# Softplus by Tanh and Ln, the gate's shares by Tanh, in a planned two-stream mixture-of-experts kernel

## The reference

```
q = softplus(gelu(x @ q_w1.T + q_b1) @ q_w2.T + q_b2)      # k likewise
z = 1 / (sum over c of q*k_sum * SCALE + dim);  A = q^T k;  out = (A v^T * SCALE + v) * z
...
top_val, top_idx = top_k(xf @ gate_w + gate_b, 2)          # 24 experts
prob = softmax(top_val)                                    # two numbers per token
out += prob[expert] * (gelu(xf @ w1 + b1) @ w2 + b2)       # exact gelu, per expert
```

## Time and profile before

| | us |
|---|---|
| three runs, median (lowest to highest) | 1048.32 (1047.94 to 1048.72) |
| span of the profiled execution | 1043.2 |
| PE busy | 905.4 (87%) |
| PE weight loads busy | 789.0 (76%) |
| DVE busy | 569.7 (55%) |
| ACT busy | 484.6 (46%) |
| POOL busy | 497.2 (48%) |

### The profile page before, as it was taken

One profiled execution on the slowest core, in us unless ns is written; L12 is line 12 of the kernel. 1 busy time (PEld: TensorE's weight loads), 2 busy tenths in 40 slices (PEclk: granted clock), 3 DMA queues, 4 the chain that ended last, 5 costly groups with the idle time before them and its releaser, 6 DMA issues.

```text
span 1043.2 us, 26677 instructions
## 1 busy us (share of the span) xinstructions
PE 905.4 (87%) x8696; PEld 789.0 (76%) x8696; DVE 569.7 (55%) x2226; ACT 484.6 (46%) x814; POOL 497.2 (48%) x519
## 2 busy tenths in 40 slices
PE   4757999998999799999999998996899999998670
PEld 2327899976889777899888898883688867888570
DVE  7897500066785065785058400588883888872112
ACT  3333544448634257734345444352528455654320
POOL 0551560271027571035372743577744657277655
PEclk9886999999999899999999999898999999999985
DMA  9765999973578783488895899944658456669982
GB/s 306 242 205 156 300 308 242 237 203 95 123 191 231 187 212 104 118 208 234 218 254 146 209 274 226 230 129 130 153 141 189 124 115 165 142 155 247 258 196 75
DMA packets 278655, 200.19 MB, mean 192 GB/s; under 512 B 146112, under 2 KB 233536, under 8 KB 278400
## 3 DMA queue, kind: packets, MB, share of 16 engines
q1 hardware_dynamic: 262144, 164.90, 63.1%
q0 software_dynamic: 16384, 33.59, 11.2%
HBM read 115.56 MB, written 55.57 MB: 164 GB/s over the span
## 4 chain that ended last, share of the span: by engine, by line
PE 58%; DVE 20%; DMA 8%; issue 5%; ACT 4%; POOL 4%; SPq 1%; DVEq 0%; POOLq 0%; ACTq 0%
PE bank L1425 20%; PE bank L1403 5%; PE bank L1405 5%; PE bank L1404 5%; DMA turned<-rows 4%; PE bank L1291 4%; POOL got L2123 3%; PE bank L1244 3%; DMA got<-y_l,slot_index 3%; PE bank L1263 2%; PE bank L1220 2%; PE bank L1253 2%; PE bank L1422 2%; DVE xn L1708 2%; PE bank L1301 2%
## 5 line engine op out<-in xcount | busy, mean ns | idle before, releaser
L1425 PE MATMUL bank<-second,hid 128*128 128x128 f32 x2560 | 369.7, 287 | 0.0
L2123 POOL DMA_INDIRECT got<-y_l,slot_index x256 | 244.7, 956 | 236.4 <-DMA y_l<-y 114.3
L1425 PEld LDWEIGHTS bank<-second,hid 128*128 128x128 f32 x2560 | 324.7, 195 | 4.7 <-issue 3.0
L2103 POOL DMA_INDIRECT rows<-rows_sent,slot_index x192 | 187.8, 978 | 282.2 <-issue 167.7
L1575 ACT ACTIVATE hid<-bank 128x512 f32<-128x512 f32 x320 | 189.7, 597 | 280.4 <-PE bank L1405 266.0
L1403 PE MATMUL bank<-turned,blocks_l 128*128 128x128 f16 x1280 | 239.7, 222 | 41.1 <-DMA turned<-rows 31.2
L1921 DVE SCALAR_TENSOR_TENSOR x_res<-got,share,x_res 128x128 f32<-128x128 f32 x256 | 77.4, 348 | 319.5 <-DMA got<-y_l,slot_index 312.9
L1405 PE MATMUL bank<-turned,blocks_l 128*128 128x128 f16 x1280 | 239.8, 223 | 0.0
L1404 PE MATMUL bank<-turned,blocks_l 128*128 128x128 f16 x1280 | 239.1, 222 | 0.0
L1403 PEld LDWEIGHTS bank<-turned,blocks_l 128*128 x1280 | 127.6, 100 | 55.4 <-issue 52.7
L1404 PEld LDWEIGHTS bank<-turned,blocks_l 128*128 x1280 | 127.1, 99 | 8.9 <-issue 5.9
(11 more groups left out here) (208 smaller groups left out, 1215.6 us busy)
## 6 DMA issues: line engine op xcount, KB each, us to landing
second<-in_w_dram SPq DMA_DIRECT2D x243, 256.0 KB, 5.3
y_l<-y SPq DMA_DIRECT2D x104, 256.0 KB
second<-in_w_dram SPq DMA_DIRECT2D x192, 128.0 KB
got<-y_l,slot_index POOLq DMA_INDIRECT x256
rows<-set SPq DMA_DIRECT2D x1, 3584.0 KB, 14.9
rows<-set SPq DMA_DIRECT2D x7, 512.0 KB, 6.4
rows<-rows_sent,slot_index POOLq DMA_INDIRECT x192
hid<-in_w_dram SPq DMA_DIRECT2D x9, 256.0 KB, 5.2
```

What stands on the lines that cost most here:

```text
L1425: m = t.do.matmul(out, hid[:, at], second[:, at], start=False, stop=(c == C - 1))
L2103: d = g.do.indirect_dma_start(rows_dram[s], at, rows[:, 2 * D * i:2 * D * i + 2 * D], None)
L2123: d = g.do.indirect_dma_start(got_mem[slot][:, col:col + D], None, y_dram[layer][s][layer.team(ev.i)], at)
```

## The change

Three things change, and the planner's table with them.

The softplus is computed as max(x, 0) - ln(0.5 - 0.5 t) with t = tanh(-|x|/2), which is the same number, since 0.5 - 0.5 t = 1/(1 + exp(-|x|)). The gap's softmax of two is computed from the Tanh of half the gap; the four DVE instructions of the shares become two. The constant 0.5 gets a column of its own among the constants. The planner's costs of ACT fall from 5.0 to 3.7 for `la_soft` and from 1.6 to 0.35 for `r_gap`, that of DVE for `r_share` from 0.8 to 0.5.

```diff
-CCOL, CCOLS = columns([("ident", P), ("rev0", L0.E), ("rev1", L1.E), ("iota", 1), ("one", 1),
+CCOL, CCOLS = columns([("ident", P), ("rev0", L0.E), ("rev1", L1.E), ("iota", 1), ("one", 1), ("middle", 1),
...
-        "r_top": [[(VE, 1.0 + 5 * n, 0.1)]], "r_gap": [[(VE, 0.2, 0.1), (SC, 1.6, 0.1)]],
+        "r_top": [[(VE, 1.0 + 5 * n, 0.1)]], "r_gap": [[(VE, 0.2, 0.1), (SC, 0.35, 0.1)]],
...
-        "r_share": [[(VE, 0.8, 0.1)]], "r_end": ...
+        "r_share": [[(VE, 0.5, 0.1)]], "r_end": ...
...
-        "la_second": [[(PE, 2.4, 0.2), (VE, 1.4, 0.1)]], "la_soft": [[(SC, 5.0, 0.15), (VE, 1.4, 0.1)]],
+        "la_second": [[(PE, 2.4, 0.2), (VE, 1.4, 0.1)]], "la_soft": [[(SC, 3.7, 0.15), (VE, 1.4, 0.1)]],
...
-                a.do.activation(gap, gap, ACT.Exp).then_inc(gap_exp[ev.s].sem, 1)
+                a.do.activation(gap, gap, ACT.Tanh, scale=0.5).then_inc(gap_tanh[ev.s].sem, 1)
...
-                    a.do.activation(mag, mag, ACT.Exp).then_inc(attn_exp[ev.s].sem, 1)
+                    a.do.activation(mag, mag, ACT.Tanh, scale=0.5).then_inc(attn_exp[ev.s].sem, 1)
...
-                    a.do.activation(mag, mag, ACT.Ln, bias=ccol("one")).then_inc(attn_exp[ev.s].sem, 1)
+                    a.do.activation(mag, mag, ACT.Ln, bias=ccol("middle"), scale=-0.5).then_inc(attn_exp[ev.s].sem, 1)
...
-                    gap, total = columns["gap"], columns["pick"]
-                    v.wait_ge(*gap_exp[ev.s].after(Ev("r_gap", *ev[1:])))
-                    then(v.do.tensor_scalar(total, gap, 1.0, None, ALU.add))
-                    then(v.do.reciprocal(total, total))
-                    then(v.do.tensor_scalar(S[:, 0, :], total, 0.5, None, ALU.mult))
-                    m = v.do.tensor_tensor(S[:, 1, :], S[:, 0, :], gap, ALU.mult)
+                    v.wait_ge(*gap_tanh[ev.s].after(Ev("r_gap", *ev[1:])))
+                    for k, slope in enumerate((-0.25, 0.25)):
+                        m = v.do.tensor_scalar(S[:, k, :], columns["gap"], slope, 0.25, ALU.mult, ALU.add)
...
-                    v.do.scalar_tensor_tensor(mem[j], bk, 0.0, mem[j], ALU.max, ALU.add).then_inc(soft_done[ev.s].sem, 1)
+                    v.do.scalar_tensor_tensor(mem[j], bk, 0.0, mem[j], ALU.max, ALU.subtract).then_inc(soft_done[ev.s].sem, 1)
```

More of the change, by code:

```diff
@@ L207, in work @@
         "r_soft": [[(VE, 0.6, 0.1), (SC, 1.6, 0.1)]], "r_norm": [[(VE, 0.7, 0.1)]],
-        "r_top": [[(VE, 1.0 + 5 * n, 0.1)]], "r_gap": [[(VE, 0.2, 0.1), (SC, 1.6, 0.1)]],
+        "r_top": [[(VE, 1.0 + 5 * n, 0.1)]], "r_gap": [[(VE, 0.2, 0.1), (SC, 0.35, 0.1)]],
         "r_rank": [[(VE, 0.6 + 3 * n, 0.1), (PE, 0.3 + n, 0.2)]], "r_slot": [[(VE, 3.4 + 9 * n if more else 2.2 + 5 * n, 0.1)]],
         "r_page": [[(VE, 1.5, 0.1)]],
-        "r_share": [[(VE, 0.8, 0.1)]], "r_end": [[(VE, 0.5, 0.1), (PE, 0.1, 0.2)]], "r_send": [[(VE, 0.3, 0.1)]],
+        "r_share": [[(VE, 0.5, 0.1)]], "r_end": [[(VE, 0.5, 0.1), (PE, 0.1, 0.2)]], "r_send": [[(VE, 0.3, 0.1)]],
         "scatter": [[(GP, 1.27 * TOP_K * tokens, 2.2)]], "gather": [[(GP, 1.27 * TOP_K * BT, 2.4)]], "add": [[(VE, 2.4, 0.1)]],
@@ L1066, in macaron_program @@
         route_exp = signals("route_exp", SC, r_soft=1)
-        gap_exp = signals("gap_exp", SC, r_gap=1)
+        gap_tanh = signals("gap_tanh", SC, r_gap=1)
         attn_gelu = signals("attn_gelu", SC, la_qk=2, la_vg=2)
@@ L2295, in constants @@
     put("one", 1)
+    put("middle", 0.5)
     h = np.zeros((P, HCOLS), np.float16)
```

## The result

The changed kernel took 1056.97 us (median of 4 runs, 1055.07 to 1059.93), the kernel before 1048.52 (4 runs, 1047.94 to 1051.54). The ratio is 1.0086, 95% interval 1.0053 to 1.0119: slower by 0.9%. The forecast was 1051.3 us, slower by 3.0; it came to 8.5.

The account below looks back on a forecast made before the run. PE was taken to bound the kernel, ACT mattering only where PE waits. Span 1043.2 - 2.5 (seams of round 1) + 5.5 (the end) = 1046.2; the median 1048.3 + 3.0 = 1051.3 us, 8-in-10 range 1043 to 1059.

Parts of the forecast that it names:

- The loads: ACT's table loads before each Exp go; PE's softplus waits shrink by 2.6 us in stream 0 and 2.0 in stream 1.
- The first seam: Stream 0, round 1: the second ranking and first unit come 1.4 us later; PE's wait for rows grows from 6.76 to about 11.
- The end: Round 3: scatters ahead of gathers put the last ranking at 959.5 and the last team's first unit at 989.3; span +3.
- the tail: Gathers, adds and stores behind the last team's units: as before, 28.1 us.
- the forecast's own: The main case, 1051.3 us: range 1048 to 1055, chance 0.45.
- rival 3: Slower by more: second team keeps its 33.6 us and moved gathers hold up PE's turns; 1056 to 1060 us, chance 0.15.
- the seam of stream 1: Between rounds 1 and 2: rows come first, PE bounds, its 1.44 us wait goes; round 2 begins 2.5 us sooner.
- seams of round 1: The term for both streams' passage out of round 1 in the sum: -2.5 us on the span.
- two ways to the last ranking: Two estimates of when round 3's last ranking comes: 959.5, which was taken, and 957.1.
- 12 units more before it: The second estimate of the last ranking: 939.6 plus 20.0 us for twelve units less 2.5, giving 957.1.
- the first way: From the fourth batch's turn at 903.5, 56 us of PE work to the last ranking at 959.5.
- The twelve units of the last team: Last team's expert units on PE: 28.5 us taken, between 23.2 and the 33.6 of before.

Follow-up runs that it names:

- e6: The changed kernel with the planner's three old costs, so the new functions in the order of before: 1038.44 us, 0.9897 of the kernel before.
- e4: The kernel before with only the planner's r_share cost changed, 0.8 to 0.5, so the end's new order alone: 1187.72 us, ratio 1.0177.
- e7: The changed kernel with the r_share cost put back to 0.8, so round 1 as changed and the end's order as before: 1044.38 us, ratio 0.9983.
- e5: The changed kernel run again unchanged, beside the kernel before: 1054.06 us, ratio 1.0068.
- e8: As e6, with Tanh in place of the softplus's Ln, so no softplus is computed and only time counts: 1032.94 us, ratio 0.9873.
- e2: The kernel before, old functions kept, with the change's three planner costs, so the new order alone: 1190.17 us, ratio 1.0219.
- e1: The same program as e6, new functions in the order of before, in another set: 1167.36 us, 0.9987 of the kernel before.
- e9: The kernel before, in its order, with only the softplus computed by Tanh and Ln: 1163.22 us, ratio 0.9967.
- e11: The kernel before with only the planner's la_soft cost changed, 5.0 to 3.7, so round 1's new order alone: 1181.00 us, ratio 1.0108.

## Why the prediction was right in its sign and short in its size

**Right.** The two effects and their signs. The loads: 46, and the waits at the softplus get smaller; e6 shows that this reaches the end. The first seam: a wait of about 11, measured 10.31. No wait at the second. The end, where "the sign is decided": ranking to first unit 29.8 (29.86), a wait of some 21 (18.35), the tail 28.1 (28.2). e4 and e7 show that this wait is the order's, and e7 what it costs: 9.7 us. The times from the start fit too, POOL free at 872 (872.8), gathers done at 892 (893.0), the fourth batch turned at 903.5 (904.70), but that they fit to 1.2 us is in part luck: in e5, the same program, the batch is turned at 910.68.

**Near the edge.** The time of 1056.97 lies in the range of 8 in 10 (1043 to 1059) but above the forecast's own (1048 to 1055), where rival 3 had 0.15 for 1056 to 1060 "if the ranking comes after 963"; it came at 964.27. That rival's reasons hold in part: the last team kept 31.5 of its 33.6 us, and one turn (894.08) waits 1.50 us for its tokens where 0.56 were waited at 879.23 before, but the turn of the fourth batch (904.70) waits for nothing.

**Mis-sized: the loads.** PE's waits at the softplus were to shrink by 4.6, 2.6 in stream 0 and 2.0 in stream 1. They shrank by 3.3 (2.1 and 1.3), in e5 by 2.3, and with the order of before (e6) by 5.7. The new order puts other waits for ACT in the place of the old ones.

**The step that failed** is the seam of stream 1: "-2.5, which is what round 2 begins with", in the sum "- 2.5 (seams of round 1)". Counted from the start, round 2 did begin 3.0 us sooner (534.07 for 537.07), but by the luck of an early start: this profile was 4.2 ahead at the first softplus, and e5, which wasn't, begins round 2 at 540.30. Counted from the first softplus on (231.76 before, the Tanh at 227.60 after and at 232.82 in e5) round 2 begins 1.2 us later than before, and 2.2 later in e5. Its first turn hangs on the last `l2` of the round by a chain of its own: store of `y`, gathers, add, norm. That took 29.1 us before (507.98 to 537.07) and 30.1 after (503.97 to 534.07), while PE had 309 or 310 matmuls to do in it, 26.0 us of work before and 24.1 after. So the idle time only moved, from the seam (1.44) to the turn (1.40 to 5.88). And PE came out of it at half clock: 4.4 us, by the rows above. The last ranking of round 2, at 735.65 before, came at 736.35 and in e5 at 741.33; from the first softplus on that is 4.9 us later than before, and 4.6 in e5, by the only profile that there is of the kernel before. From the start it is +0.7 where -2.5 stood, 3.2 us off, and the 3.2 would be more without the early start. The prediction asked what is late next at the first seam and not at the second. e7 has the same order and the same wait (5.77); e6 with the order of before waits 0.35 at the first turn (528.18) and 2.41 at the second.

**Mis-sized: the end.** The prediction had two ways to the last ranking, and the second was "12 units more before it", 20.0 us. PE between the last ranking of round 2 and the last one, two sums over four stretches each, before and then after:

```profile
sum 203.97, PE 194.64 PEld 161.31 DVE 161.62 ACT 111.46 POOL 115.53; mean PE 48.66 PEld 40.33 DVE 40.41 ACT 27.86 POOL 28.88
```

```profile
sum 227.92, PE 216.38 PEld 182.65 DVE 168.15 ACT 124.47 POOL 131.67; mean PE 54.09 PEld 45.66 DVE 42.04 ACT 31.12 POOL 32.92
```

They cost 23.95 us, 21.7 of it busy and 2.2 idle. That is 1.81 a unit, where I took 1.67 from two units at 135 us. Those belong to L0; three `l2` of L1 in a row stand at 955.20, 956.98 and 958.76 before, 1.78 apart. 957.1 + 3.2 + 4.0 = 964.3 is where the ranking came; against the 959.5 that I took it is 4.8 late. On the first way, the one that I took, the fourth batch was turned 1.2 late, and from there it was 59.6 us instead of 56.

The twelve units of the last team took 31.5 us, 28.5 was forecast. Waits of 1.58 and 2.53 stay, and the clock was 0.50 and then 0.87 for the first 10 us, which by the same estimate is 0.50 x 4.87 + 0.13 x 5 = 3.1 us. That is as much as the term was short by. But the 28.5 was a choice between 23.2 and 33.6 and had no clock and no wait in it by name, so that the clock alone is the difference isn't shown. (Its lower bound was off too: 23.2 counts twelve steps of 1.67 where the 30.2 beside it counts eleven.)

4.8 + 3.0 are the 7.6 by which the span of 1046.2 was short, but for 0.2: the steps themselves end at 1045.9. The median was short by less, 1056.97 - 1051.3 = 5.7, since the profile of before was of a faster execution than I took it for.

So of the slower clock an estimated 4.4 us stand at the turn and 3.1 at the last team. The prediction took each wait at its length and had nothing for what comes behind it. The trace of before had it to be read: behind the wait of 6.76 the granted clock is 0.72 over 10 us, 2.8 us on top of the wait.

**On the table sets.** The Trainium skill, "ScalarE: Activation LUTs", section "Table sets: the hidden batching unit", lists tanh with exp and with sigmoid and names none in the row of the gelu set. Its word "separate" there is said of the gelu's approximations, so that a Tanh after a gelu needs a load was my reading of the table. The trace doesn't agree with that reading: Tanh at 227.60 follows the gelu of 227.10 with no load, and in e8 gelu, Tanh, Tanh and the copy stand in a row. The Trainium skill's section "What ACT_TABLE_LOAD costs" on the same page has 1380 ns of draining with a load. That isn't seen here either: the Tanh ends at 228.74, the load at 228.75 takes 1.28, and the Ln starts at 230.05.

**Open.** Functions and order do not add up across sets: e6 has -1.0%, e2 has +2.2%, and the changed kernel +0.7 to +0.9%; e1, in one set with e2, has -0.1%. The changed kernel wasn't in that set, and how much of the gap is the set's stays open. In the set of e5 to e8 the order alone, without the new functions, wasn't run. Nor was it tried whether the planner could be given the true costs and yet be kept from the late ranking.

## What to carry to other kernels

A planner's cost is part of the kernel's order: when an operation gets cheaper, put the new number in and leave it out, and time both. Here the functions gave up to 1.0%, and one number that went from 0.8 to 0.5 in the table took as much away. The version to keep is the changed functions with the old costs: 1038.44 us, 0.9897 (0.9867 to 0.9927) of the kernel before, in e6; in e1 it couldn't be told from it.

When time is saved ahead of a chain of transfers, follow the chain to where PE next waits, and price that wait with the slow clock behind it, not by its length alone. What gets later is read from the last link that nothing can hide, here the last ranking: 24 us of other work went from behind it to ahead of it, PE had 11.5 us left to do in a chain of 29.9, and the rest of the chain is the wait of 18.35 before the last team.

## What the runs showed of the chip that I had not expected

**A wait costs more than its length.** I read PE's waits of 2.2 us or more from 300 us on in six profiles (before, after, e5 to e8). Behind each of the 33 over 3.0 us the granted clock of the next 5 us was between 0.50 and 0.73; behind those of 2.27, 2.39 and 3.00 it was 1.00, behind the six others of 2.2 to 2.8 it was 0.50 to 0.69. A longer wait didn't mean a longer stretch at 1.2 GHz: behind 10.31 the first 5 us had 0.71, behind 5.88 they had 0.50.

**The same program took 12% longer in another set, in part by gaps on PE.** e1 and e6 are one program, 1167.36 and 1038.44 us. The group of the experts' second matmuls in e1, and then in e6:

```profile
L1425 PE MATMUL bank<-second,hid 128*128 128x128 f32 x2560 | 378.9, 290 | 13.4 <-issue 13.3
```

```profile
L1425 PE MATMUL bank<-second,hid 128*128 128x128 f32 x2560 | 370.7, 287 | 0.0
```

In e1 PE stands still ahead of matmuls that wait for nothing the profile shows, in pieces of up to 1.2 us (19 of them are the 13.3); its busy time is 948.8 us for 904.6 and its span 1159.6 for 1039.0, so idle time has some 76 of the 121 us and busy time 44. The kernels beside it in e1 to e4 and e9 to e11 show the same, and e9 to e11 ran on the chip of e5 to e8, so the chip alone doesn't make them. What does isn't settled.
